# Where the engines branch to one of two attention paths: after the graph layer's last norm, or inside it

## The reference, cut to what matters

```python
def layer0(x, adj):                      # graph layer
    h = gat(x, adj, W1, a1)              # softmax over masked scores, times Wh
    h = gat(h, adj, W2, a2)
    h = layernorm(x + h)
    ff = relu(h @ w_ff1 + b_ff1) @ w_ff2 + b_ff2
    return layernorm(h + ff)             # the last norm

def layer1(src, adj):                    # attention layer, 8 heads of 16
    attn = softmax(q @ k.T / 4)
    out = sum((attn * (adj == r)) @ v[r] for r in range(4))
    x = layernorm(src + out @ Wo + bo)
    return layernorm(x + gelu(x @ W1 + b1) @ W2 + b2)

return layer1(layer0(x, adj), adj)
```

## Time and profile before

| What | Value |
|---|---|
| Median of 3 runs | 1142.9 us (1141.55 to 1143.61) |
| The profiled execution's own time | 1141.11 us |
| Its span, first to last instruction | 1139.3 us |
| Busy: PE, DVE, ACT, POOL | 91%, 82%, 62%, 49% of the span |
| Mean granted TensorE clock | 0.988 of full speed |
| Graph layer, up to the last write of `xs` | 0 to 385 us |
| Attention and feed-forward | 387 us to the end |

### The profile page before, as it was taken

How to read it: one execution, slowest core, us unless ns; L and a number is a source line. 1 busy time by engine, 2 the same in 40 slices (tenths; PEclk the granted TensorE clock), 3 DMA queues, 4 the chain that set the end, 5 groups by cost and what they waited for, 6 DMA issues and landing times. The chain is left out here.

```text
span 1139.3 us, 20494 instructions
## 1 busy us (share of the span) xinstructions
PE 1037.4 (91%) x5765; PEld 488.7 (43%) x5765; DVE 932.3 (82%) x2320; ACT 705.4 (62%) x1323; POOL 563.4 (49%) x506
## 2 busy tenths in 40 slices
PE   3588889888888799999999999999999999999997
PEld 3557667576664233333333333333333333244443
DVE  4898998989987778887888888888888888748787
ACT  2476777767765456665666666666666665654443
POOL 3112112121111388877887888888888887700000
PEclk9899999999999899999999999999999999999999
DMA  7131211312031313331433143223313330000001
GB/s 227 61 111 56 98 70 56 111 57 90 22 113 64 92 49 106 108 102 35 119 93 88 59 116 97 67 81 107 101 49 103 106 79 2 1 10 29 37 28 46
DMA packets 49279, 86.85 MB, mean 76 GB/s; under 512 B 8376, under 2 KB 35256, under 8 KB 44219
## 3 DMA queue, kind: packets, MB, share of 16 engines
q1 hardware_dynamic: 47018, 85.59, 24.6%
q10 hardware_dynamic: 2192, 0.47, 0.2%
HBM read 52.19 MB, written 29.36 MB: 72 GB/s over the span
## 5 line engine op out<-in xcount | busy, mean ns | idle before, releaser
L1597 DVE TENSOR_REDUCE top<-b_peak 128x1 f32<-128x512 f32 x488 | 320.3, 684 | 73.9 <-PE b_peak L1273 72.6
L1438 ACT ACTIVATE b_prob<-b_score 128x1024 f32<-128x1024 f32 x256 | 258.1, 1025 | 151.9 <-PE b_score L1288 106.2
L1787 POOL TENSOR_TENSOR b_picked<-b_prob,mask 128x512 f32<-128x512 f32 x192 | 234.2, 1240 | 58.1 <-ACT b_prob L1438 45.8
L1787 POOL TENSOR_TENSOR b_picked<-b_prob,b_mask 128x512 f32<-128x512 f32 x185 | 226.1, 1243 | 56.6 <-ACT b_prob L1438 46.1
L1064 POOL TENSOR_TENSOR a_hw_n<-a_hw,a_inv 128x512 f32<-128x512 f32 x16 | 16.7, 1043 | 221.7 <-issue 168.4
L804 ACT ACTIVATE a_att<-a_att,a_least 128x512 f32<-128x512 f32 x128 | 91.4, 715 | 32.4 <-DVE a_least L834 32.4
L1273 PE MATMUL b_peak<-b_k_stack,b_q_stack 96*128 96x512 bf16 x256 | 98.4, 384 | 6.6 <-DVE top L1597 6.2
L1273 PE MATMUL b_peak<-shared 96*128 96x512 bf16 x232 | 90.0, 389 | 7.5 <-DVE top L1597 4.0
L834 DVE CUSTOM_DVE_ANT_0 a_att<-a_att,a_no_edge 128x512 f32<-128x512 f32 x128 | 87.3, 700 | 0.0
L550 PE MATMUL a_mid<-a_h_t,wff 128*128 128x512 f32 x128 | 64.9, 626 | 14.4 <-ACT a_hid L798 12.8
L1288 PE MATMUL b_score<-shared 98*128 98x512 bf16 x256 | 77.3, 383 | 0.0
(11 more groups left out here) (230 smaller groups left out, 1891.9 us busy)
## 6 DMA issues: line engine op xcount, KB each, us to landing
a_adj_in<-in_adj SPq DMA_DIRECT2D x15, 1024.0 KB, 5.1
scratch<-shared SPq DMA_DIRECT2D x32, 384.0 KB, 3.0
shared<-scratch SPq DMA_DIRECT2D x16, 768.0 KB, 6.9
scratch<-shared SPq DMA_DIRECT2D x32, 256.0 KB, 2.1
b_q_stack<-scratch SPq DMA_DIRECT2D x8, 768.0 KB, 5.5
b_k_stack<-scratch SPq DMA_DIRECT2D x8, 768.0 KB, 8.2
a_x_t<-in_x_t SPq DMA_DIRECT2D x16, 256.0 KB, 2.6
xs<-in_x SPq DMA_DIRECT2D x16, 256.0 KB, 5.3
```

The costliest lines, as they stand in the source:

```text
L1438: act.activation(prob[s % 2][:, 2 * u:2 * u + 2, :], score[u][:, :, :], ACT.Exp, scale=float(DH) ** -0.5).then_inc(sem("exp_ready"), 1)
L1597: dve.tensor_reduce(top[g][:, hh, c:c + 1], peak[hh % 2][:, :], AX.X, ALU.max, negate=True).then_inc(sem("peak_read"), 1)
L1787: pool.tensor_tensor(picked[(NR * s + rel) % 2][:, hh, :], prob[s % 2][:, hh, :], m, ALU.mult).then_inc(sem("picked_pool"), 1)
```

## The change

PE, ACT and DVE now branch earlier. What was left of each engine's graph-layer tail at that place is put into a function, `ending`, and called as the first thing of both paths. For PE that is the last four peaks and `turn_n`; for ACT `rstds`, `centre` and `keep_x`; for DVE six maxima and `norm_shift`. DVE's flag is read earlier too: before the maxima 18 and 19 rather than between 21 and 22. SP and POOL are not touched.

```diff
@@ tensor
                 peaks(18, 20)
                 load_flag(pe, "tensor")
+
+            def ending():
                 peaks(20, 24)
                 turn_n(B - 1)
+            endings["tensor"] = ending
@@ scalar
                 load_flag(act, "scalar")
+
+            def ending():
                 rstds(1, B - 1)
                 centre(B - 1)
                 keep_x(B - 1)
+            endings["scalar"] = ending
@@ vector
                 most(16, 18)
                 norm_stats(1, B - 1)
                 norm_mean(1, B - 1)
+                load_flag(dve, "vector")
+
+            def ending():
                 most(18, 20)
                 norm_shift(B - 1)
-                most(20, 22)
-                load_flag(dve, "vector")
-                most(22, 24)
+                most(20, 24)
+            endings["vector"] = ending
@@ attention, tensor: in run(path, rels)
+                endings["tensor"]()
+                peaks_read(pe)
                 turns(pe, turn, last)
-            peaks_read(pe)
             both_paths(pe, "tensor", run)
@@ attention, scalar: in run(path, rels)
+                endings["scalar"]()
+                peaks_read(act)
                 turns(act, turn, last)
-            peaks_read(act)
             both_paths(act, "scalar", run)
@@ attention, vector: in run(path, rels)
+                endings["vector"]()
                 turns(dve, turn, last)
             both_paths(dve, "vector", run)
```

More of the change, by code:

```diff
@@ L430, in graph_layer @@
         ctx.enter_context(nc.allow_non_contiguous_dma(reason="a few hundred values, once"))
-        flags = {}
+        flags, endings = {}, {}
         def load_flag(eng, name):
@@ L1073, in _, with attention @@
             load_flag(pool, "gpsimd")
-        return flags, x_kept
-def attention(nc, block, z, w, xs, codes, flags, x_kept, scratch, first_qk, sem, shared, out, keep):
+        return flags, endings, x_kept
+def attention(nc, block, z, w, xs, codes, flags, endings, x_kept, scratch, first_qk, sem, shared, out, keep):
     with ExitStack() as ctx:
@@ L2021, in build @@
             w["wff1"][0], w["wff2"][0] = sb("wff1_0", [P, z.F], till=first), sb("wff2_0", [P, z.FC, z.D], till=first)
-            flags, x_kept = graph_layer(nc, block, z, w, io, xs, codes, other, general, flagged, shared, first_qk, sem, keep)
-        attention(nc, block, z, w, xs, codes, flags, x_kept, scratch, first_qk, sem, shared, out, keep)
+            flags, endings, x_kept = graph_layer(nc, block, z, w, io, xs, codes, other, general, flagged, shared, first_qk, sem, keep)
+        attention(nc, block, z, w, xs, codes, flags, endings, x_kept, scratch, first_qk, sem, shared, out, keep)
 def kernel(**inputs):
```

## The result

The changed kernel takes 1146.8 us (median of 10 runs, 1143.0 to 1148.79); the kernel before, run beside it, 1142.45 us (10 runs). The ratio is 1.0036, 95% interval [1.0026, 1.0046], so it is slower by 0.36%, about 4.3 us. The profiled execution took 1146.19 us with a span of 1144.4 us and a mean clock of 0.983; that of before 1141.11, 1139.3 and 0.988.

The account below looks back on a forecast made before the run. PE was taken as the bound (91% busy, 9.69 of 10 us in attention). PE's stand 2.75 (attention's 0.1 counted within) plus half clock 1.2 gave +4.0 us on 1142.9: 1146.9, range 1142.4 to 1149.4.

Parts of the forecast that it names:

- DVE's restart: DVE stands before maximum 18 for flag load (0.85) plus branch (2.8): 3.55 us later, 0.85 to 4.15 by the bounds.
- rival D: Worse: the half clock lasts, or DVE's path needs a second block (1.0 to 3.4 us more): +7 or more, chance 0.06.
- Start of attention: PE's first attention peak waits for DVE's last maximum: about 387.4 instead of 387.32, +0.1 us.
- The load: SP's load of `b_k_stack` for graph 1: issued at 390.2, landing 9.1 us later, at 399.3.
- The stand at the stacks: PE at graph 1's first peak, reached at about 396.7, stands for `b_k_stack` until 399.4: +2.75 us.
- Half clock: After PE's stand, 2.5 to 3.5 us of its work at 1.2 GHz costs 1.2 to 1.8; 1.2 taken.
- Given back: Delay recovered after PE's stand at graph 1's stacks: none counted in the main case.
- main case: DVE's delay makes the stacks late, PE stands, half clock follows: +4.0 us (+2.3 to +6.5), 1146.9, chance 0.58.
- rival B: The delay is real but given back at PE's stand for the stack, no half clock: 1.9 us, 1144.8, chance 0.10.
- ACT and POOL: ACT's later roots and POOL's first product at about 391.6 both come before they are needed: no cost.
- Rival A: DVE's branch costs only its record, 0.07 us; `x_kept` 0.9 us late: 0 to +0.5, 1143, chance 0.18.
- Rival C: Branches nearly free and PE not waiting for the stack; PE and DVE move 2.5 us forward: 1140.4, chance 0.08.

Follow-up runs that it names:

- before_late: The kernel before with no branch moved, SP loading the small tile of ones twice and waiting for each, so the stack loads are late: 1146.07 us, ratio 1.0031.
- dve_only: The changed kernel with only DVE's branch moved, PE and ACT branching where the kernel before does: 1147.71 us, ratio 1.0051.
- after_mid: The changed kernel with SP starting graph 1's stack loads after 20 maxima, no longer after the write of `xs`: 1144.0 us, ratio 1.0016.
- after_shift40: The changed kernel with 40 more semaphore increments at the start of DVE's program, where they are executed: 1146.46 us, ratio 1.0038.
- pe_only: The changed kernel with only PE's branch moved, ACT and DVE branching where the kernel before does: 1140.96 us, ratio 0.9995.
- after_pad40: The changed kernel with 40 more semaphore increments at the start of DVE's path 1, which is jumped over: 1146.09 us, ratio 1.0041.
- after_early: The changed kernel with SP starting graph 1's stack loads after 18 maxima, no longer after the write of `xs`: 1146.74 us, ratio 1.0045.
- before_early: The kernel before, no branch moved, with SP starting graph 1's stack loads after 18 maxima: 1145.08 us, ratio 1.003.

## Why the prediction was right, and where its sizes were off

The forecast was slower, 1146.9 us, and the measured median is 1146.8. As a difference it was +4.0 us on a kernel before of 1142.9, and 4.3 were measured on 1142.45. The mechanism held step by step: PE's branch hidden, DVE's exposed, the norm's chain late, `x_kept` and with it the stacks late, PE standing for the DMA, half clock behind it. before_late shows that the second half of this chain makes the loss by itself, dve_only that DVE's branch starts it, and after_mid that the loss shrinks when the loads don't hang on the chain. The agreement to 0.1 us is luck in part, since the base was 0.45 us too high and several terms were off and cancelled:

- **DVE's restart: 3.55 us predicted, 4.63 measured.** The flag's load was taken as 0.85, from a place where it wasn't interrupted, and is 1.3; the branch was taken as 2.8 and is 3.5. after_shift40 shows that about 0.8 us of the difference is one more block of code, fetched because of where these instructions happen to lie. Without it the branch is 3.1, and in pe_only 2.9, close to the 2.8 that "PE's price less the shorter block" had given. The upper bound of 4.15 was too low: it allowed for a longer branch, not for a second block, which was only in rival D.
- **Start of attention: +0.1 predicted, +1.33 measured.** The term is DVE's: with 1.08 us more there the transposes come at 387.74 instead of 386.6, and the first peak behind them.
- **The load: 9.1 us predicted, 8.2 measured.** This gave 0.9 us back. A time to landing isn't a constant: from 7.8 us (after_pad40) to 9.7 us (after_early) were seen for the same 768 KB.
- **The stand at the stacks: +2.75 predicted, +2.97 measured,** since the errors of DVE (+1.08) and of the load (-0.9) nearly cancel.
- **Half clock: +1.2 predicted, +2.46 measured.** I had PE's work at half clock for 2.5 to 3.5 us, of which only the lower end had a row near it (the 2.5 us of the earlier trace rows with a clock of 0.56). The clock is low for 6.8 us, of which PE works 5.1 us behind the stand. Half of that is 2.5. The size is that of one execution: the four traces with such a stand have 1.6, 1.6, 2.46 and 3.1 us, all above the 1.2.
- **Given back: 0 predicted in the main case, 0.76 measured** between 401 and 540 us. It comes at two places, 0.25 us at 511 us and 0.5 us at 520 us, where the loop over the turns begins. There the kernel before waits a little for DVE, and the changed kernel doesn't. This is rival B's kind of thing in size, but not by its mechanism: it isn't at turn 0. The 0.25 us also appear in dve_only and before_early, where PE's branch isn't moved. The 0.5 us at 520 appear in every kernel with PE's branch moved and in none of the three without, so they go with it. It may be code position again; that was only argued.
- **ACT and POOL** cost nothing, as predicted. ACT's branch took 2.6 us (2.8 predicted). POOL's first product was at 392.73 (391.6 predicted), ahead of need.

Rival A, a branch at the price of its record, is refuted by every kernel in which DVE stands behind its branch: the smallest price there is 2.9 us, with a record of 0.07. The prediction speaks of four short records that agree with the rule of 108 ns; the earlier trace rows has three, of 45 to 72 ns, and on DVE the record isn't the price. The Trainium skill, "Advanced Engine Details and Errata", section Control Flow Timing, gives about 108 ns for a compare-and-branch; the measurement decides, and none of the branches of PE, ACT or DVE to their path was that cheap here. The Trainium skill, "Runtime: NRT & Kernel Launch", section Instruction fetch mechanics, has the stall of a taken branch until its target's page is fetched, and the traces agree: 3.4 to 4.0 us on PE. Rival C fell with A. Of rival D both conditions came, and smaller than it had them: the second block on DVE at 0.8 us instead of 1.0 to 3.4, and the half clock, which lasted 6.8 us in the profiled execution.

Still open: why the changed kernel's lag grows by another 0.7 us between 1049 and 1127 us, in the feed-forward part (in after_shift40 it grows by 0.1), and what sets the rate of the stack loads.

## What to carry to other kernels

Here a branch over the code of a whole path cost 2.6 to 4.0 us on PE, ACT and DVE, whatever its record said, so put such a branch where that engine is already waiting, and not ahead of an instruction on which another engine's chain hangs. When a delay is moved off one engine, look for the transfer whose issue hangs on the delayed chain: here 4.7 us later in its issue became 3 us of PE's time, and the half clock behind it added 2.5. And before starting a big load earlier, check what small fetches run beside it.

## What the runs showed of the hardware that was not expected

- A branch to a path whose code had to be fetched cost 2.6 to 4.0 us with the DMA engines nearly idle (share up to 0.07 beside the branches of PE and DVE), and 6.3 to 6.6 us with them full: PE 3.40 to 3.99 against 6.51 (before_early), DVE 2.9 to 3.7 against 6.3 (after_early), POOL at most 2.8 (the changed kernel) against 6.6 (after_mid). Blocks of code are listed on queues of the same 16 DMA engines as the data. SP is the exception: in the changed kernel its branch is taken at 390.6 and its next transfer issued at 390.93. Whether its target had to be fetched was not looked at.
- On PE the record of the branch holds the stall. On ACT, DVE and POOL it doesn't (54, 72 and 45 ns throughout).
- Forty instructions more ahead of a branch made DVE's stand 0.8 us shorter, with one block less to fetch.
- The clock's low stretches differ between executions of nearly the same code: behind the stand for the stacks 3.4 us (after_pad40, after_shift40) or 6.8 us (the changed kernel, before_late).
